# A gated cross-attention and mixture-of-experts block: layer norms by pairs of batches, and routed tiles two steps ahead

## The reference

```python
x = x + tanh(g_xattn) * attention(q=layernorm(x), k=v=ctx)   # one head, d=128, with Wo, bo
h = layernorm(x)
shared = silu(h @ w1) * (h @ w2) @ w3
s = sigmoid(h @ router_w); top 2 of s + expert_bias; gate = s at these two
routed = sum over experts of gate * (silu(h @ w1e) * (h @ w2e) @ w3e)
x = x + tanh(g_ffn) * (shared + routed)
```

## Time and profile before

| | us |
|---|---|
| median of 3 runs | 74.22 (73.93 to 74.92) |
| the profiled execution | 73.88 |
| its span, first to last instruction | 72.2 |
| PE / DVE / ACT / POOL busy | 60.9 / 38.8 / 26.0 / 11.7 |
| mean granted TensorE clock | 0.985 |

### The profile page before, as it was taken

The page is one execution under the profiler, slowest core; times in us unless marked ns, Lnnn a source line. Parts: engine busy times, 40 slices in busy tenths (PEclk is TensorE's granted clock), DMA queues, the critical chain, the costliest instruction groups (busy, mean ns, idle before and its releaser), DMA issues.

```text
span 72.2 us, 1153 instructions
## 1 busy us (share of the span) xinstructions
PE 60.9 (84%) x341; PEld 42.9 (60%) x342; DVE 38.8 (54%) x159; ACT 26.0 (36%) x71; POOL 11.7 (16%) x26
## 2 busy tenths in 40 slices
PE   1997998596979995999999999999999999996200
PEld 0335877574744564576984577475676998884100
DVE  2074824688332259833569795864730398765300
ACT  0334858043738930044411323031156823332000
POOL 4005099804100000140000000000005260000000
PEclk9999999999999999999999999999999999999985
DMA  0898470000000000000000000610698300000560
GB/s 0 229 321 203 119 313 24 0 0 0 0 0 9 0 0 5 0 0 0 0 0 0 0 0 5 189 37 0 198 283 250 145 5 0 0 0 5 148 157 13
DMA packets 5084, 4.80 MB, mean 66 GB/s; under 512 B 336, under 2 KB 4816, under 8 KB 5072
## 3 DMA queue, kind: packets, MB, share of 16 engines
q1 hardware_dynamic: 3984, 3.93, 17.8%
q10 hardware_dynamic: 1088, 0.74, 3.6%
HBM read 4.15 MB, written 0.52 MB: 65 GB/s over the span
## 4 chain that ended last, share of the span: by engine, by line
PE 72%; DVE 9%; DMA 4%; issue 3%; ACT 3%; POOL 1%; DVEq 0%; POOLq 0%
PE bank L944 15%; PE bank L927 15%; PE bank L928 14%; DMA x_sb<-in_x_dram 4%; PE bank L831 3%; PE bank L827 3%; PE bank L1013 3%; PE bank L822 2%; PE bank L965 2%; PE bank L836 2%; PE bank L848 2%; PE bank L1005 2%; PE bank L1004 2%; DVE hid L648 2%; PE bank L807 1%
## 5 line engine op out<-in xcount | busy, mean ns | idle before, releaser
L648 DVE TENSOR_TENSOR hid<-silu_t,bank 128x512 f32<-128x512 f32 (+1 forms) x13 | 8.4, 645 | 9.8 <-ACT silu_t L484 8.5
L484 ACT ACTIVATE silu_t<-bank 128x512 f32<-128x512 f32 (+1 forms) x13 | 7.3, 563 | 15.3 <-PE bank L928 15.3
L944 PEld LDWEIGHTS bank<-shared_sb,hid 128*128 128x128 f32 x64 | 8.1, 191 | 3.7 <-issue 1.9
L944 PE MATMUL bank<-shared_sb,hid 128*128 128x128 f32 x64 | 8.7, 280 | 0.9 <-DVE hid L648 0.9
L927 PE MATMUL bank<-x2nT,shared_sb 128*128 128x512 f32 x16 | 8.3, 603 | 0.6 <-ACT x2nT L475 0.6
L928 PE MATMUL bank<-x2nT,shared_sb 128*128 128x512 f32 x16 | 8.2, 592 | 0.0
L376 POOL TENSOR_TENSOR rstd<-var_eps,neg_half 128x4 f32<-128x4 f32 x4 | 4.1, 1018 | 21.3 <-DVE var_eps L557 21.3
L807 PE MATMUL bank<-warm_rows 128*128 128x512 bf16 x14 | 5.3, 530 | 1.6 <-DVE warm_rows L578 1.5
L410 POOL TENSOR_TENSOR acc<-acc,gated 128x512 f32<-128x512 f32 x2 | 2.5, 1270 | 24.9 <-ACT gated L494 24.9
L928 PEld LDWEIGHTS bank<-x2nT,shared_sb 128*128 128x128 f32 x16 | 3.0, 190 | 3.8 <-issue 3.8
L944 PEld LDWEIGHTS bank<-dense_w,hid 128*128 128x128 f32 x32 | 4.1, 191 | 1.9 <-issue 1.0
(11 more groups left out here) (135 smaller groups left out, 103.1 us busy)
## 6 DMA issues: line engine op xcount, KB each, us to landing
tile_w<-in_routed_w_dram SPq DMA_DIRECT2D x8, 192.0 KB, 3.6
shared_sb<-in_shared_w_dram SPq DMA_DIRECT2D x1, 768.0 KB, 4.5
dense_w<-in_routed_w_dram SPq DMA_DIRECT2D x2, 192.0 KB, 2.5
params<-in_attn_params_dram ACTq DMA_DIRECT2D x1, 265.0 KB, 4.1
ctx_sb<-in_ctx_dram SPq DMA_DIRECT2D x1, 256.0 KB, 4.0
x_sb<-in_x_dram SPq DMA_DIRECT2D x1, 256.0 KB, 5.6
ctx_sb<-in_ctx_dram ACTq DMA_DIRECT2D x1, 256.0 KB, 5.8
out_dram<-acc SPq DMA_DIRECT2D x1, 256.0 KB, 2.6
```

The source lines that it names most:

```text
L484: nc.scalar.activation(silu_t[:, k % 2, columns(k)], bank[up_bank(k)][:, columns(k)], ACT.Silu).then_inc(silu_ready, 1)
L648: nc.vector.tensor_tensor(hid[:, k % HID_RING, columns(k)], silu_t[:, k % 2, columns(k)], bank[up_bank(k) + 1][:, columns(k)], ALU.mult)\
L944: last = nc.tensor.matmul(down_bank(k, b)[:, b * P:(b + 1) * P], hid[:, k % HID_RING, b * P:(b + 1) * P], down_weights(k), start=first and ...
```

## The change

Front: the first half of both norms is done in two pairs instead of four blocks at once (`PARTS`, three semaphores for x and for x2nT). In TensorE's queue the ones_row matmul of the fused bias goes behind attention_scores(0), turn_probs(1) ahead of attend(0), the transposes of xn's second half ahead of value_output(1), the transposes of x2n's pair 0 ahead of attention_scores(2), and the five keep_warm matmuls there are dropped (the ten at the start stay). The first share_up runs pair by pair. Of x2n's block 2 DVE takes over the normalisation. DVE does values(1) after the row maxima, and share(0) ahead of add_attention(2).

Tail: after share_down(10) tiles 2 to 7 run in three steps of two (two ups, then the two downs of the step before), and chunks 11 and 12 come behind them, with banks 2 and 3 as further up banks, bank 5 as a third down bank, and chunk 12 in banks 6 and 7. The store of the first half is issued when all tiles have been added.

The core of the diff, indentation cut by eight:

```diff
     BY_POOL = DENSE
-    ADDITIONS = [("chunk", 10), ("tile", 0), ("tile", 1), ("chunk", 11)] + [("tile", t) for t in range(2, ALWAYS)] + [("chunk", 12)] \
+    ADDITIONS = [("chunk", 10)] + [("tile", t) for t in range(ALWAYS)] + [("chunk", 11), ("chunk", 12)] \
...
+PARTS = (slice(0, 2), slice(2, 4), slice(4, 8))
...
 def up_bank(k):
-    return 2 + 4 * (k % 2) if k < FIRST_PAIR else 2
+    return 2 + 4 * (k % 2) if k < FIRST_PAIR else (2, 6)[k - FIRST_PAIR]
 def tile_up_bank(t):
-    return bank[6 + t % 2][:, 0:2 * P]
+    return bank[(6, 7, 2, 3, 6, 7, 6, 7)[t] if t < ALWAYS else (6, 7)[t % 2]][:, 0:2 * P]
 def tile_down_bank(t):
-    return bank[t % 2][:, 0:D]
+    return bank[(0, 1, 5)[t % 3] if t < ALWAYS else t % 2][:, 0:D]
...
     sp.dma_start(ctx_sb[:, halves(0), :], c_dram[:, halves(0), :]).then_inc(ctx_loaded[0], 16)
-    sp.dma_start(x_sb[:, halves(1), :], x_dram[:, halves(1), :]).then_inc(x_loaded[1], 16)
-    sp.wait_ge(x_loaded[1], 16)
+    sp.dma_start(x_sb[:, halves(1), :], x_dram[:, halves(1), :]).then_inc(x_loaded[2], 16)
+    sp.wait_ge(x_loaded[2], 16)
...
     more_groups(0)
-    sp.wait_ge(added, added_before[("chunk", CHUNKS - 1)])
+    sp.wait_ge(added, added_before[("chunk", FIRST_PAIR)])
     sp.dma_start(o_dram[:, halves(0), :], acc_blocks[:, halves(0), :]).then_inc(stored, 16)
+    sp.wait_ge(added, added_before[("chunk", FIRST_PAIR + 1)])
...
     pool.memset(ones_row[:, :], 1.0).then_inc(consts_ready, 1)
-    def inverse_deviation(n, h):
-        pool.wait_ge(var_ready, 2 * n + h + 1)
-        pool.tensor_tensor(rstd[:, n, halves(h)], var_eps[:, n, halves(h)], neg_half[:, :], ALU.pow)\
+    def inverse_deviation(n, m):
+        pool.wait_ge(var_ready, 3 * n + m + 1)
+        part = PARTS[m]
+        pool.tensor_tensor(rstd[:, n, part], var_eps[:, n, part], neg_half[:, 0:part.stop - part.start], ALU.pow)\
...
     pool.wait_ge(consts_ready, 2)
-    inverse_deviation(0, 0)
-    inverse_deviation(0, 1)
-    pool.wait_ge(rstd_ready, 2)
+    for m in range(3):
+        inverse_deviation(0, m)
+    pool.wait_ge(rstd_ready, 3)
...
     nc.scalar.activation(tanh_g[:, :], gains, ACT.Tanh).then_inc(tanh_ready, 1)
-    def normalise(h):
-        act.wait_ge(shift_ready, h + 1)
-        for b in (HALF * h + 2, HALF * h + 3):
+    def normalise(blocks, shifted):
+        act.wait_ge(shift_ready, shifted)
+        for b in blocks:
...
     copy_g(3)
-    normalise(0)
+    normalise((3,), 1)
     act.wait_ge(x2n_pair_turned, 2)
-    nc.scalar.copy(x2nT[:, 256:512], bank[7][:, 0:256]).then_inc(x2nT_ready[0], 1)
+    nc.scalar.copy(x2nT[:, 256:512], bank[7][:, 0:256]).then_inc(x2nT_ready[1], 1)
...
     gate_dense(9)
-    rare_silu(0)
-    rare_silu(1)
+    for t in range(ALWAYS):
+        rare_silu(t)
     share(11)
-    for t in range(2, ALWAYS):
-        rare_silu(t)
...
             nc.vector.bn_stats(stats[:, n, k, :], src[:, k, :]).then_inc(stats_ready, 1)
-    def moments(n, h):
-        for b in range(HALF):
-            k = HALF * h + b
+    def moments(n, m):
+        part = PARTS[m]
+        for k in range(part.start, part.stop):
...
             nc.vector.bn_aggr(mean_var[:, n, k, :], stats[:, n, k, :]).then_inc(moments_ready, 1)
-        dve.wait_ge(moments_ready, B * n + HALF * (h + 1))
-        nc.vector.tensor_scalar(var_eps[:, n, halves(h)], mean_var[:, n, halves(h), 1], EPS, None, ALU.add)\
+        dve.wait_ge(moments_ready, B * n + part.stop)
+        nc.vector.tensor_scalar(var_eps[:, n, part], mean_var[:, n, part, 1], EPS, None, ALU.add)\
             .then_inc(var_ready, 1)
-    def shifts(h):
-        dve.wait_ge(rstd_ready, 2 + h + 1)
-        nc.vector.scalar_tensor_tensor(shift[:, halves(h)], mean_var[:, 1, halves(h), 0], -1.0, rstd[:, 1, halves(h)],
+    def shifts(m):
+        dve.wait_ge(rstd_ready, 3 + m + 1)
+        nc.vector.scalar_tensor_tensor(shift[:, PARTS[m]], mean_var[:, 1, PARTS[m], 0], -1.0, rstd[:, 1, PARTS[m]],
...
     nc.vector.memset(warm_rows[:, :], 0.5).then_inc(warm_ready, 1)
-    dve.wait_ge(x_loaded[0], 16 * 2)
-    block_stats(0, x_sb, range(HALF))
-    moments(0, 0)
-    dve.wait_ge(rstd_ready, 1)
-    normalise(0, x_sb, xn, range(HALF), xn_by_dve)
-    dve.wait_ge(x_loaded[1], 16)
+    for m in range(2):
+        dve.wait_ge(x_loaded[m], 16)
+        block_stats(0, x_sb, range(2 * m, 2 * m + 2))
+        moments(0, m)
+    for m in range(2):
+        dve.wait_ge(rstd_ready, m + 1)
+        normalise(0, x_sb, xn, range(2 * m, 2 * m + 2), xn_by_dve)
+    dve.wait_ge(x_loaded[2], 16)
     block_stats(0, x_sb, range(HALF, B))
-    moments(0, 1)
+    moments(0, 2)
...
     attention_scale(0)
-    add_attention(0)
-    second_stats(0)
-    add_attention(1)
-    second_stats(1)
-    moments(1, 0)
-    values(1)
-    shifts(0)
+    for p in range(2):
+        add_attention(p)
+        second_stats(p)
+        moments(1, p)
+    dve.wait_ge(rstd_ready, 4)
...
     dve.wait_ge(x2n_pair_turned, 1)
-    nc.vector.tensor_copy(x2nT[:, 0:256], bank[6][:, 0:256]).then_inc(x2nT_ready[0], 1)
+    nc.vector.tensor_copy(x2nT[:, 0:256], bank[3][:, 0:256]).then_inc(x2nT_ready[0], 1)
+    shifts(1)
+    normalise(1, x2, x2n, (2,), x2n_by_dve)
...
     row_maxima(3)
+    values(1)
...
                                        acc[:, bass.ds(to, D)], ALU.mult, ALU.add).then_inc(added, 1)
+    share(0)
     add_attention(2)
-    share(0)
+    second_stats(2)
     add_attention(3)
-    second_stats(2)
...
     share(1)
-    moments(1, 1)
-    shifts(1)
+    moments(1, 2)
+    shifts(2)
...
     add_dense(10)
+    for t in range(2, ALWAYS):
+        rare_hid(t)
+        add_rare(t - 2, to[t - 2])
     share(11)
-    add_rare(0, to[0])
-    add_rare(1, to[1])
-    rare_hid(2)
-    rare_hid(3)
+    add_rare(ALWAYS - 2, to[ALWAYS - 2])
+    add_rare(ALWAYS - 1, to[ALWAYS - 1])
+    share(12)
     add_dense(11)
-    add_rare(2, to[2])
-    for t in range(4, ALWAYS):
-        rare_hid(t)
-        add_rare(t - 1, to[t - 1])
-    share(12)
-    add_rare(ALWAYS - 1, to[ALWAYS - 1])
...
             pe.wait_ge(x2n_by_dve, 2)
+            pe.wait_ge(x2_ready, HALF)
         else:
-            pe.wait_ge(x2n_by_act, 2)
+            pe.wait_ge(x2n_by_dve, 3)
+            pe.wait_ge(x2n_by_act, 1)
         for b in (2 * p, 2 * p + 1):
-            last = nc.tensor.transpose(bank[6 + p][:, (b % 2) * P:(b % 2 + 1) * P], x2n[:, b, :], ident[:, :])
+            last = nc.tensor.transpose(bank[(3, 7)[p]][:, (b % 2) * P:(b % 2 + 1) * P], x2n[:, b, :], ident[:, :])
...
     def turn_x2n_second():
-        pe.wait_ge(x2n_by_dve, 4)
-        pe.wait_ge(x2n_by_act, 4)
+        pe.wait_ge(x2n_by_dve, 5)
+        pe.wait_ge(x2n_by_act, 3)
...
-    def fused_bias():
-        pe.wait_ge(consts_ready, 2)
-        pe.wait_ge(rows_loaded, 16)
-        pe.wait_ge(vo_w_ready, 1)
-        nc.tensor.matmul(bank[6][:, P:2 * P], bv_col.to_broadcast([P, P]), woT[:, :], start=True, stop=False)
-        nc.tensor.matmul(bank[6][:, P:2 * P], ones_row[:, :], bo_row, start=False, stop=True).then_inc(fused_done, 1)
...
     query_key(0)
-    fused_bias()
+    pe.wait_ge(vo_w_ready, 1)
+    nc.tensor.matmul(bank[6][:, P:2 * P], bv_col.to_broadcast([P, P]), woT[:, :], start=True, stop=False)
...
     attention_scores(0)
+    pe.wait_ge(consts_ready, 2)
+    pe.wait_ge(rows_loaded, 16)
+    nc.tensor.matmul(bank[6][:, P:2 * P], ones_row[:, :], bo_row, start=False, stop=True).then_inc(fused_done, 1)
...
     turn_probs(0)
+    turn_probs(1)
...
     attend(0)
-    turn_probs(1)
...
     attend(1)
+    pe.wait_ge(xn_by_pool, HALF)
+    turn(bank[4], xn, 1, xn_turned)
...
     value_output(1, range(HALF)).then_inc(vo_done, 1)
-    pe.wait_ge(xn_by_pool, HALF)
-    turn(bank[4], xn, 1, xn_turned)
...
     query_key(3)
-    keep_warm(2, 7)
+    turn_x2n_pair(0)
...
     attention_scores(3)
-    keep_warm(3, 7)
-    pe.wait_ge(vo_ready[1], 1)
-    turn_x2n_pair(0)
...
     def share_up(k):
-        if k >= 2:
-            pe.wait_ge(hid_ready, k if k > FIRST_PAIR - 1 else k - 1)
+        if k >= FIRST_PAIR:
+            pe.wait_ge(r_hid_ready, (4, ALWAYS)[k - FIRST_PAIR])
+        elif k >= 2:
+            pe.wait_ge(hid_ready, k - 1)
         h = half_of(k)
-        pe.wait_ge(x2nT_ready[h], 2 - h)
+        pe.wait_ge(x2nT_ready[1 + h], 1)
...
+    def first_share_up():
+        w1, w2 = up_weights(0)
+        for p in range(2):
+            pe.wait_ge(x2nT_ready[p], 1)
+            c = slice(256 * p, 256 * p + 256)
+            nc.tensor.matmul(bank[up_bank(0)][:, c], w1, x2nT[:, c], start=True, stop=True)
+            last = nc.tensor.matmul(bank[up_bank(0) + 1][:, c], w2, x2nT[:, c], start=True, stop=True)
+        last.then_inc(up_done, 1)
...
             pe.wait_ge(tile_gates_ready, 1)
-        if k >= FIRST_DENSE + DENSE:
-            if k < CHUNKS - 1:
-                pe.wait_ge(gated_ready, HALF * (k - FIRST_DENSE - 1))
-            else:
-                pe.wait_ge(added, HALF)
+        if k == 10:
```

(60 more changed lines are left out.)

## The result

The changed kernel takes 70.35 us (median of 4 runs, 70.3 to 71.16); the kernel before took 74.08 in the same runs (73.8 to 74.92). The ratio is 0.954, 95% interval 0.950 to 0.959: faster by 4.6%. The profiled execution has a span of 68.6 us, 3.6 less than before, where 68.3 was forecast.

A forecast was written before the change was run, and what follows sets the result against it. Idle time at both ends was taken as the only gain, TensorE being fully busy in the middle. 72.2 - 2.9 - 0.9 - 0.1 = 68.3 us span, plus 1.68 and 0.34: 70.3; range 69.3 to 72.0, its own 69.5 to 71.0.

The forecast's parts named there:

- rival 3: The front's gain is given back in the middle by a wait that was hidden: 73.2 us; chance 0.04.
- The front, 2.9: From the start to share_down(2): norms by pairs and new queue orders gain 2.9 us, between 0.3 + 0.41 and 4.5.
- the second: Fused bias: ones_row matmul (0.41) behind attention_scores(0) leaves query_key(1)'s path; -0.7 at the scores' start, -0.8 at attend(0).
- The first step: Layer norm of x by pairs: first pair's xn at 6.4 against 6.98, -0.3 at query_key(0).
- -1.3 and -2.1: Both turn_probs ahead of attend(0): attend(1) ends 1.3 sooner; turn(xn) ahead of value_output(1): query_key(2) starts 2.1 sooner.
- The tail, 0.9: After share_down(10): ups run two ahead, so hid(12) ends at 65.5 against 66.40; 0.9 us, bounds -0.2 and +1.2.
- Rival 2 (Vector binds): The tail gives nothing because Vector's in-order steps bind: 71.2 us; chance 0.13.
- The end, 0.1: Stores: the 256 KB store leaves two microseconds ahead, the last may find engines freer; 0.1 us, between 0 and 0.5.
- Rival 1 (the norms collide): In both norms, Vector's first-pair normalise and GpSimd's second pow wait for each other: 71.1 us; chance 0.17.

The follow-up runs named there:

- norm 1 by four: The changed kernel with the first norm's blocks 0 to 3 through one var_eps and one 128x4 pow, as before: 70.91 us, ratio 0.960.
- the bank experiment: The changed kernel with tiles 6 and 7 up into banks 2 and 3, chunk 11 into 6 and 7, chunk 12 into 2 and 3: 69.93 us.
- nine warm-ups: The changed kernel with nine instead of ten warm-up matmuls at the start: 70.04 us, ratio 0.949.

## Why the prediction was right, and where its terms were off

Forecast 70.3, measured 70.35, within the range and the forecast's own. The mechanism holds: the idle time lay at both ends, the middle moved as a block (23.14 to 23.20 in every kernel, so rival 3 falls), and the granted clock held: 0.994 in the mean, and in the run without keep_warm 1.00 from 18 to 21 us. So rival 4, to which 0.04 was given (the granted clock falls without keep_warm, and the kernel gets slower), falls too. The terms:

- **The front, 2.9, measured 2.37.** The step that failed is the second: the ones_row matmul "off the path" for -0.7 at the scores and -0.8 at attend(0). It only moved from ahead of query_key(1) to between the two scores, where it fills a wait and both scores pay an exposed fill. attend(0) starts at 13.11, -0.3, and the run that moved it back cost 0.1. The walk left 0.76 us for the two scores together (from query_key(1)'s end, 9.97 before, less 0.7, so 9.27, to 11.35 - 0.91 = 10.44, less 0.41 for the matmul between them); they take 0.54 + 0.64 = 1.18. That is 0.4 of the 0.5 by which attend(0) is late. The first step was right in itself (0.3 by the run with norm 1 by four), but fused weights ended at 7.0 in the profiled execution and not at 6.7. At the front's end the stalled share_down(2) adds a little: it takes 1.16 where the kernel before has 1.01. Of the 2.37, the parts that were undone alone account for about 1.9 (norm 1 0.2 to 0.3, the ones_row matmul 0.1, keep_warm 0.64, norm 2 1.0, turn_probs 0); first_share_up, the order of the transposes and Vector's order were not tried alone.
- **From attend(0) to the end of pair 1's transposes** the walk gave 19.1 - 12.6 = 6.5 us; measured 19.54 - 13.11 = 6.43. Here Vector's sum was the right one to make. Of the -1.3 and -2.1 that I gave to TensorE's new order (both turn_probs, turn(xn) first) about -0.8 and -1.8 are seen in its queue (query_key(2) starts at 15.9), but nothing at the end comes of the first of them; the second wasn't tried alone.
- **pow on two blocks** was taken at 1.03. It takes 0.70 to 0.72 for 128x2, and 1.01 to 1.05 on four. It lay off the path, as the walk had it, so the sum didn't suffer.
- **share_down(2)** was to stall for hid(2), and did: until 31.43, where 31.05 was forecast.
- **The tail, 0.9, measured 0.70.** The wait at ups 6 and 7 was seen, as 0.35; it is 0.5 with its exposed fills. Rival 2 (Vector binds) falls by the bank experiment.
- **The end, 0.1, measured 0.5.** The early store's share was right; the rest, a last store that lands sooner, was not foreseen, and its cause stays open.
- **Rival 1 (the norms collide)** falls. Vector's normalise ran beside the pow:

```profile
5.51 0.70 POOL L382 TENSOR_TENSOR rstd<-var_eps,neg_half 128x2 f32<-128x2 f32 x1
5.52 0.35 DVE L572 TENSOR_SCALAR xn<-x_sb,mean_var,rstd 128x128 f32<-128x128 f32 x1
```

The pow runs from 5.51 to 6.21, the normalise of block 0 starts at 5.52 and takes 0.35, where it takes 0.34 in the kernel before, with no pow beside it. Neither waited for the other. The second norm has the same: Vector's two normalises run from 16.84 to 17.44 and GpSimd's pow from 17.01 to 17.73, at 0.34 each and 0.72, again with neither behind the other.

So misses of 0.5 us in the front and of 0.2 in the tail were in part made up by 0.4 at the end, which leaves the span 0.3 longer than forecast (68.6 against 68.3). The last 0.3 was luck: I had added 0.34 because the median of the kernel before lay so far above its profiled execution, and for the changed kernel that distance is 0.05 (70.35 against 70.30). The forecast of the sum was better than that of its terms.

## What to carry to other kernels

When a matmul is moved out of a gap, ask what filled the gap: in a stretch where each step waits for another engine, taking it out saves little (0.1 of 0.41 us here), since the wait that it covered stays, and the steps around it pay an exposed fill (0.1 to 0.3 us each here) that back-to-back ones don't. Follow the chain to the engine that is last, and shorten that engine's work (here Vector's norm, 1.0 us) before reordering the others' queues. And in-order queues hide cheap gains: a silu and a product whose input was there (share_up(2) ends at 27.8, its silu ran at 30.1) stood behind a 1 us wait for GpSimd, and two free banks stood beside two busy ones; these two edits of a few lines took 0.76 and 0.50 us off their stretches.

## What the runs showed of the hardware that I had not expected

The warm-up matmuls at the start take 0.44 us each, where matmuls of the same shape later take 0.22. Two views of the changed kernel, the window there (granted clock third from the end) and the chain:

```profile
1.50:3.60 2.10, 2.07 (x5) 0.72 (x6) 0.00 (x0) 0.68 (x1) 0.22 (x3) 1.00 0.61 179
...
4.50:5.40 0.90, 0.90 (x4) 0.29 (x2) 0.86 (x6) 0.00 (x0) 0.62 (x1) 1.00 1.09 310
```

The column says 1.00, and ten matmuls of 512 bf16 columns take 4.45 us (1.53 in the chain above), 0.44 each; in the earlier trace rows three of the same shape take 0.65, 0.22 each, and the column says 1.00 there too. TensorE was idle until 1.53. So in the profile's first microseconds the granted clock doesn't tell these two durations apart, and the step from one to the other is to be read from matmuls of equal shape. I took the step for a rise of the clock, and the expectation for nine warm-ups calls it that; no view shows what makes it. The step comes sooner in one execution than in another: the same ten take 3.85 to 4.45 us. With the params landing at nearly the same time (4.0 and 4.1 us from issue) the first transposes start at 6.61 with ten in 4.00 us and at 7.03 with ten in 4.45, so the step seems to move the whole kernel by some 0.4 us, and the landing of the params, 3.8 to 4.9 us, by as much again in the latest executions.
